# Two top-2 stages written out straight, and the third attention step in another order

## The reference

```python
# layer 0: windows of 8x8 tokens, 4 heads of 16, shifted by 4
x = x + _L0_conv_ref(_ln_c(x), ...)      # norm over channels, qkv, softmax(q k^T * scale + bias), proj

# layers 1 and 3: top-2 of 8 experts
def _L1_ffn_ref(x, router_w, router_b, expert_w, expert_b):
    router_probs = jax.nn.softmax(x @ router_w + router_b, axis=-1)
    top_p, top_i = jax.lax.top_k(router_probs, 2)
    top_p = top_p / jnp.sum(top_p, axis=-1, keepdims=True)
    expert_out = jnp.einsum('bnd,edc->bnec', x, expert_w) + expert_b
    gathered = jnp.take_along_axis(expert_out, top_i[..., None], axis=2)
    return jnp.einsum('bnk,bnkc->bnc', top_p, gathered)
```

## Time and profile before

| | us |
|---|---|
| median of 3 runs | 6426.1 (6420.86 to 6432.86) |
| profiled execution | 6420.26 |
| its span in the profile | 6418.5 |
| attention, first top-2 stage, last top-2 stage (windows) | 1094, 670, 788 |
| busy share of the span: PE, DVE, ACT, POOL | 80%, 67%, 57%, 18% |

### The profile page before, as it was taken

How to read it: one execution, slowest core, us unless ns; L and a number is a source line. 1 busy time by engine, 2 the same in 40 slices (tenths; PEclk the granted TensorE clock), 3 DMA queues, 4 the chain that set the end, 5 groups by cost and what they waited for, 6 DMA issues and landing times. The chain is left out here.

```text
span 6418.5 us, 134286 instructions
## 1 busy us (share of the span) xinstructions
PE 5130.1 (80%) x47166; PEld 3325.4 (52%) x47166; DVE 4332.3 (67%) x9746; ACT 3666.3 (57%) x6942; POOL 1151.3 (18%) x1068
## 2 busy tenths in 40 slices
PE   7887887637968886699969998407999999948887
PEld 4664664223533332499969995203555555523332
DVE  6886887975348887722223346697777777758886
ACT  5675665746547774622243324456677767747664
POOL 2332333043210001500000000131121111121110
PEclk9998998857989998599989999758999999979998
DMA  1111111423338886300000124237666666547777
GB/s 33 34 31 31 35 34 51 107 72 85 105 119 275 271 272 205 98 0 0 0 0 0 53 97 126 68 104 99 81 83 83 82 80 80 67 127 244 237 234 222
DMA packets 794232, 646.13 MB, mean 101 GB/s; under 512 B 496551, under 2 KB 644199, under 8 KB 793779
## 3 DMA queue, kind: packets, MB, share of 16 engines
q1 hardware_dynamic: 792755, 639.06, 40.6%
q0 software_dynamic: 1024, 1.05, 0.1%
HBM read 549.78 MB, written 90.20 MB: 100 GB/s over the span
## 5 line engine op out<-in xcount | busy, mean ns | idle before, releaser
L2367 PE MATMUL sw_pC<-sw_row,sw_wc 128*128 128x128 f32 x10160 | 1158.5, 275 | 56.1 <-DVE sw_row L2242 54.9
L2367 PEld LDWEIGHTS sw_pC<-sw_row,sw_wc 128*128 128x128 f32 x10160 | 1147.3, 192 | 58.2 <-DVE sw_row L2242 55.5
L2801 PE MATMUL sp_pC<-sp_work,sp_bands 64*64 64x512 f32 (+11 forms) x14592 | 986.3, 428 | 43.7 <-issue 43.7
L2230 DVE SCALAR_TENSOR_TENSOR sw_row<-sw_pC,sw_y 128x128 f32<-128x128 f32 x1016 | 337.9, 333 | 791.1 <-PE sw_pC L2367 791.1
L2801 PEld LDWEIGHTS sp_pC<-sp_work,sp_bands 64*64 64x64 f32 x14592 | 601.4, 133 | 431.8 <-issue 364.9
L2740 ACT ACTIVATE sp_pC<-sp_pC,sp_par 128x512 f32<-128x512 f32 x832 | 597.7, 740 | 372.3 <-PE sp_pC L2801 348.6
L1781 DVE TENSOR_TENSOR t_z<-t_z,t_ht 128x1024 f32<-128x1024 f32 x512 | 626.6, 1272 | 87.0 <-DMA t_z<-gate_rows 44.9
L1944 PE MATMUL t_pO<-t_z,t_ew 128*64 128x512 f32 x2048 | 531.1, 638 | 113.5 <-DVE t_z L1781 110.1
L2299 ACT ACTIVATE sw_y<-sw_row 128x128 f32 (+1 forms) x762 | 265.3, 348 | 592.3 <-DVE sw_row L2230 592.3
L2697 DVE TENSOR_TENSOR sp_work<-sp_work,sp_pC 128x512 f32<-128x512 f32 x512 | 351.5, 688 | 170.1 <-ACT sp_pC L2740 169.7
L307 POOL TENSOR_TENSOR wa_sc<-wa_sc,wa_sm 128x1024 f32<-128x1024 f32 x128 | 243.5, 1902 | 728.7 <-DVE wa_sm L396 728.7
(11 more groups left out here) (380 smaller groups left out, 9900.2 us busy)
## 6 DMA issues: line engine op xcount, KB each, us to landing
t_z<-gate_rows SPq DMA_DIRECT2D x512, 512.0 KB, 7.8
sp_bands<-windows SPq DMA_DIRECT2D x128, 512.0 KB
c_spent<-tokens SPq DMA_DIRECT2D x128, 256.0 KB, 2.7
cb_xs<-tokens SPq DMA_DIRECT2D x128, 256.0 KB, 2.9
wa_xs<-in_x SPq DMA_DIRECT2D x64, 256.0 KB, 2.8
tokens<-wa_xt SPq DMA_DIRECT2D x128, 128.0 KB, 1.9
tokens<-cb_h SPq DMA_DIRECT2D x64, 256.0 KB, 3.1
t_xs<-tokens SPq DMA_DIRECT2D x32, 512.0 KB, 10.9
```

What stands on the lines that cost most here:

```text
L2230: dve.scalar_tensor_tensor(row[par][c][:, :, PAD:PAD + P2], pC[c][:, 0:2 * P2].rearrange("p (b w) -> p b w", b=2), 0.0, line(sweep, c, i), ...
L2367: ins = pe.matmul(pC[c][:, 0:2 * P2], wc[:, sweep, m, :], row[1 - par][c][:, :, m:m + P2], start=(m == 0), stop=(m == 4))
L2801: ins = pe.matmul(out[halves[to], :, low * lo:low * hi], band[halves[k], (NV * g + j) % BANDS, q, AT[k][tap], :], v[halves[k], :, low * at ...
```

## The change

Three edits. In attention's step `j == 2`, ScalarE's `log(n + 1, 1)` and `root(n + 1)` move behind `save_qk` and `save_values`, and TensorE's `variance(n + 1, 1)` moves behind `qkv` and `values`. In both top-2 stages `over_beats` loses its hardware loop: all 32 beats are written out on TensorE, VectorE and ScalarE, and on GpSimd, which takes part in the last stage alone (`join`). All their waits are then for constants.

```diff
@@ attention, ScalarE
                 def body(s, j, after, back1, back2):
-                    if j == 2 and not last:
-                        log(n + 1, 1)
-                        root(n + 1)
                     if j == 3 and not first:
                         save_turned(n - 1, (k - 1) % 2, 0)
                     if after:
                         save_qk(*after[0:2])
                     if back2:
                         save_values(back2[0])
+                    if j == 2 and not last:
+                        log(n + 1, 1)
+                        root(n + 1)
                     if j == 1 and not last:
                         square(n + 1, 1)
                     exponential(s, j)
@@ attention, TensorE
                 def body(s, j, after, back1, back2):
                     scores(s)
-                    if j == 2 and not last:
-                        variance(n + 1, 1)
                     if after:
                         qkv(after[0], after[1], after[3], after[2])
...
                     if back2:
                         values(*back2[0:2])
+                    if j == 2 and not last:
+                        variance(n + 1, 1)
                     if back1:
                         turn_probs(*back1[0:2])
@@ top-2
-        def over_beats(eng, body, link=None, per=0):
-
-            for n in range(2):
-                body(Beat(n, n, 0))
-            loops = (NB - 4) // 6
-            with eng.Fori(0, loops) as t:
-                if link:
-                    link.enter(t, 6 * per)
-                for i in range(2, 8):
-                    body(Beat(6 * t + i, i % 6, t + i // 6))
-            if link:
-                link.leave(loops)
-            for n in range(2 + 6 * loops, NB):
+        def over_beats(eng, body):
+
+            for n in range(NB):
                 body(Beat(n, n % 6, n // 6))
...
-            over_beats(dve, beat, link, 3 + 11 + 1 + 3)
+            over_beats(dve, beat)
```

## The result

The changed kernel takes 6348.2 us (median of 4 runs, 6347.3 to 6355.0) against 6426.5 us before: a ratio of 0.9881, 95% interval 0.9865 to 0.9897. The profiled execution has a span of 6346.6 us, 71.9 less than before.

A forecast was written before the change was run, and what follows sets the result against it. Attention was held by a Ln-variance-Ln ping-pong and half-rate TensorE, the first top-2 stage by the DMA queue, the last by compute and jumps. 43 + 9 + 2 = 54 us off gave 6372 us, range 6350 to 6400.

The forecast's parts named there:

- exponential 1 to 2: Attention strip: distance from step 1's exponential to step 2's, 9.80 us in strip 5, forecast to come 1.24 us earlier.
- The rival of a clock that does not recover: Attention: TensorE's half-rate stretches come again, so attention gives 22 us, total 33, 6393 us; chance 0.20.
- a `variance` that comes too late: Attention: at half rate variance ends 3.2 us later, costing 1.7 us a strip, 51 over 30, 6466 us; chance 0.06.
- I take 2 us: First top-2 stage: gain chosen for writing out the loop, between 1 us lost and 5.5 us gained.
- 19.46 us for a saturated beat: First top-2 stage: distance of two z issues; if every beat takes it, twenty take 389.2 us, 1 us lost.
- 19.12: First top-2 stage: us per beat between jumps if three jump beats take 20.94; twenty then take 382.4, 5.5 gained.
- the prediction's own bracket: First top-2 stage: the range over twenty beats, from 1 us lost to 5.5 us gained.
- The other two give 2 x 4.4 = 9 us: Last top-2 stage: second and third jumps cost 4.4 us each, so writing out the loop gains 9 us; bounds 0 to 17.6.
- The first jump was worth 0: Last top-2 stage: removing the first jump's 5.5 us stall is handed back whole to the finished image's issue.
- TensorE's and ScalarE's jumps cost it little: Top-2 stages: reading that only VectorE's back jumps, 6 to 7 us three times a stage, leave much idle time.
- Constant waits and longer code: Top-2 stages: dropped register instructions and straight-code fetches each costed at nothing; a late fetch would cost 4.4 to 8.2 us.
- the low end: Whole run: 6350 us, the range's lower edge, meant to take in the near-side rival of 6358 us.

The follow-up runs named there:

- e7: Kernel before the change with only ScalarE's part of the attention edit (log and root behind save_qk and save_values): 6519.7 us, attention 1196.2 us.
- e5: Kernel before the change, loops kept, with x loads in the first top-2 stage cut to one of eight token groups from the seventh batch: stage 663.4 us.
- e6: Kernel before the change with the same short x loads as e5 and the first top-2 stage written out: stage 647.9 us.
- e4: Kernel before the change with only VectorE's program written out in both top-2 stages: ratio 0.9977; first stage 659.2 us, last 759.8 us.
- e10: Kernel before the change with only ScalarE's program written out in the last top-2 stage: stage 766.4 us, one profiled execution.
- e9: Kernel before the change with VectorE's and ScalarE's programs written out in the last top-2 stage: stage 748.8 us, one profiled execution.
- e3: Kernel before the change with only the last top-2 stage written out, on all its engines: ratio 0.9983, stage 748.9 us.
- e12: Kernel with all changes, SP's queue reordered (gates before x load and store; last stage's image behind next gates): ratio 0.9859, 6333.9 us.
- e11: Kernel before the change with only TensorE's program written out in the last top-2 stage: stage 770.4 us, one profiled execution.
- e8: Kernel before the change with only TensorE's part of the attention edit (variance behind qkv and values): 6459.9 us, attention 1135.0 us.

## Why the prediction was right or wrong

**Attention: right, the size 10% low.** Forecast 8.56 us for exponential 1 to 2, measured 8.57; full rate in all strips, as assumed; 47.4 us instead of 43. What was short is the next distance: 6.87 us were forecast (6.37 plus 0.5 for `write_h` in front of the row sums), 6.76 came, 0.11 x 30 = 3 us. The stage itself scatters: with the old order it took 1096.1 to 1104.1 us in eight profiled executions and 1110.0 in one, mean 1101.3; with the new order 1051.1 to 1052.9 in three. By the means the gain is 49.5. The rival of a clock that does not recover is refuted: no half-rate time is left between exponentials 1 and 2. The rival of a `variance` that comes too late did not happen in the pair, but its way of failing, an order in which each engine waits for the other's queue, is what the halves show: e7 loses 95 us of attention against the mean, 3.2 a strip, where the rival had priced 1.7.

**First top-2 stage: the mechanism right, the term mis-sized, 2 instead of 8.4 (5 by the means).** That the DMA queue would swallow most of the 20 us of idle time is shown by e5 and e6. The step that failed is "I take 2 us", between 19.46 us for a saturated beat and 19.12 worked out from the rest. The 19.46 was a single pair of rows; saturated beats scatter from 18.4 to 19.9 us and average 19.00. With the average the sum is 387.9 - 380.1 = 7.8 us for these two profiles. The 4.9 us of the means lie at the other end of the prediction's own bracket, 5.5.

The average of the z issues also hid something. In the loop the lag from gates to z fell from 9.3 to 5.5 us over the twenty beats, so the gates, which go at the engines' pace, took 391.7 us and not 387.9. By TensorE's mixing the beats of the loop took 18.6 us but for the first, the three of the jumps (27.2, 23.6 and 24.3 us) and their neighbours (18.4 to 18.9). So the queue set hardly a beat there: it fell behind, and each stall let it catch up. Written out, 18.64 us is still the rule, but a third of the beats take 18.7 to 20.8, when z is late.

**Last top-2 stage: the term mis-sized, 9 instead of 17.2 (16 by the means).** The step that failed is "The other two give 2 x 4.4 = 9 us". It prices the jump beats and puts the beats between them at nothing. The first jump was worth 0, as forecast: 2.71 us of waiting became 9.46. The other two gave about the 4.4 us each that the sum has, but only because both engines' stalls went. The reading "TensorE's and ScalarE's jumps cost it little" was wrong for ScalarE: VectorE's jumps alone give at most 4 us (e4), ScalarE's alone none (e10), the two together 14 (e9, 748.8 us beside the mean of 763.2). The sum looked at VectorE's idle list only. I had not looked for who else was late in the same beat; here that mistake did no harm, as both were removed.

For the rest, 7 to 8 us, there was no term. In the 24 beats of the old loop, windows before and after (us, busy by engine, granted clock, DMA share, GB/s):

```profile
5751.00:6283.00 532.00, 444.97 (x2133) 177.00 (x2131) 462.98 (x1200) 366.43 (x744) 93.06 (x48) 0.94 0.78 240
```

```profile
5694.00:6212.00 518.00, 430.14 (x2144) 174.16 (x2144) 455.15 (x1204) 363.79 (x745) 99.04 (x48) 0.97 0.79 246
```

TensorE's granted clock is higher over the same work, 0.97 for 0.94, and its busy time 15 us less. In the profile before, several beats outside the jumps and images took 21.4 us, in the profile after 20.4 is the rule. All profiles agree on when this comes: TensorE's half-rate time in the 32 beats is 40 to 48 us in the four kernels in which neither VectorE nor ScalarE jumps (all changes, e3, e9, e12), and 64 to 84 us in the ten in which at least one of them does, e4, e10 and e11 among them. So removing both jumps is what lowers it. That it works through TensorE standing without work behind the stalls fits e8 and the stretch at 0.54 in e4, but it does not explain the beats far from a jump, and no run sets the clock apart from the stalls, so this part stays argued.

**The rules.** The Trainium skill ("Runtime: NRT & Kernel Launch", section on instruction fetch mechanics) says that a taken branch outside the held pages stalls for a fetch. The traces agree: the stalls are gone in every engine that is written out. Taken as the time to be gained, the 39 us of stalls are too much: 25.6 us came back in the two stages (21 by the means), since other waits stood behind them.

**Constant waits and longer code: right, nothing.** No sequencer stood still in straight code (0.5 us of issue idle in the last stage, none in the first), and beats do not fall below 18.6 us where compute sets them: 18.64 in e6 and e12, against 18.60 in the loop. The peeled beats, which the prediction read as 18.60 too, take 18.64.

**The range.** 6350 to 6400 missed by 2 us. All three terms came out above their middles, and the low end held one such case at a time, not their sum; the last stage's missing 7 to 8 us alone would have put the result inside. By the means of the stages the three gains are 50, 5 and 16 us, 71 together.

## What to carry to other kernels

A stall that is removed is worth what the next wait leaves of it, and three cases of that stood side by side here: behind VectorE's jumps was the DMA queue in one stage (5 to 8 of 20 us came back), the image's issue in another beat (0 of 6), and ScalarE's own jump in others (at most 4 us in the stage with one engine, 14 to 16 with both). So list all engines' stalls around a jump, not the longest, and take the rhythm of a queue from twenty beats and not from one pair. And where two engines hand a small result to and fro, move both sides or neither: each half of the attention change lost 35 to 95 us, the pair gained 50.

## What the runs showed of the hardware

A back jump left VectorE without instructions for 4.2 to 8.3 us, over all profiles with its loop, and ScalarE for 2.0 to 3.7 us, the latter in the last stage alone, where a pass of its loop has 413 instructions in place of 313; TensorE's jump never did. In the first stage of the kernel before, the branches are at 2053.9, 2172.8 and 2289.6 us; the first packet of the kind "instruction" behind each begins 6.3, 4.2 and 4.9 us later and takes 0.3 us, and VectorE's sequencer goes on 1.8 us after it began. So most of a stall lies ahead of that packet. Why it begins so late is not shown; with 0.45 MB less a beat in the queue (e5) the stalls were 6.0 to 6.6 us, no shorter.

A DMA rhythm is not its bytes alone: with the same transfers in another order, so that no wait for a landing fell at the end of the queue, the beat went from 19.0 to 18.64 us. Eight strided image transfers of 512 KB each held SP for 14 to 18 us while it issued them.
